# The decay of a state-space block computed as an absolute difference in PSUM, with the z gates moved and the preparation reordered

## What is computed

```python
def _ssd(xh, dt, A, Bm, Cm):
    cum = jnp.cumsum(dt * A, axis=1)
    diff = cum[:, :, None, :] - cum[:, None, :, :]
    decay = jnp.where(mask[None, :, :, None], jnp.exp(diff), 0.0)
    scores = jnp.einsum('bln,bsn->bls', Cm, Bm)[..., None] * decay * dt[:, None, :, :]
    return jnp.einsum('blsh,bshp->blhp', scores, xh)

def _mamba2(x, ...):
    z, xBC, dt = split(x @ Win)      # xBC: causal conv of 4 taps, silu; dt: softplus
    y = _ssd(xh, dt, A, Bm, Cm) + rev(_ssd(rev(xh), rev(dt), A, rev(Bm), rev(Cm)))
    y = y + D[None, None, :, None] * xh
    y = _rmsnorm(y * silu(z), gn_w)
    return x + y @ Wout
```

## Time and profile before

| what | value |
|---|---|
| median of three executions | 2949.18 us |
| profiled execution | 2953.49 us, its span 2951.5 us |
| blocks 0 to 7 | from about 904 us to 2929 us of the span |
| one block (the second) from its start to the start of the next | 248.4 us |
| busy in the span: TensorE, VectorE, ScalarE, GpSimd | 73%, 67%, 59%, 37% |
| mean granted clock of TensorE | 0.857 |

### The profile page before, as it was taken

How to read it: one execution, slowest core, us unless ns; L and a number is a source line. 1 busy time by engine, 2 the same in 40 slices (tenths; PEclk the granted TensorE clock), 3 DMA queues, 4 the chain that set the end, 5 groups by cost and what they waited for, 6 DMA issues and landing times. The chain is left out here.

```text
span 2951.5 us, 64266 instructions
## 1 busy us (share of the span) xinstructions
PE 2153.9 (73%) x26182; PEld 1100.1 (37%) x26182; DVE 1981.8 (67%) x2779; ACT 1744.2 (59%) x2811; POOL 1079.7 (37%) x827
## 2 busy tenths in 40 slices
PE   4277777776774887698688588658857886885886
PEld 3022222222221553354255245325524542552553
DVE  2587888888877566565666656565765666666564
ACT  1266766766653575477367457536754773674574
POOL 0044444444451343244045235304522531451342
PEclk6588888888896998799799799869978988997998
DMA  4000000000001111110111111011111101111111
GB/s 133 0 0 1 0 1 0 1 0 0 1 0 29 32 34 28 35 33 15 44 38 26 38 27 40 15 31 32 34 36 26 42 15 39 33 25 30 32 34 31
DMA packets 96695, 74.59 MB, mean 25 GB/s; under 512 B 69392, under 2 KB 77584, under 8 KB 95120
## 3 DMA queue, kind: packets, MB, share of 16 engines
q1 hardware_dynamic: 96400, 70.48, 10.0%
HBM read 20.62 MB, written 8.39 MB: 10 GB/s over the span
## 5 line engine op out<-in xcount | busy, mean ns | idle before, releaser
L892 POOL TENSOR_TENSOR SQ<-SQ 128x512 f32<-128x512 f32 x344 | 467.2, 1360 | 708.4 <-ACT SQ L811 425.1
L859 POOL TENSOR_TENSOR Y<-Z 128x512 f32<-128x512 f32 x256 | 330.8, 1292 | 531.6 <-DVE Z L1096 297.7
L807 ACT ACTIVATE O<-bank 128x512 f32<-128x512 f32 x512 | 304.3, 594 | 210.2 <-PE bank L571 207.5
L1293 DVE TENSOR_TENSOR SQ<-bank,O 128x512 f32<-128x512 f32 x344 | 236.2, 689 | 163.8 <-issue 118.8
L571 PE MATMUL bank<-SS,work 32*128 32x512 bf16 x512 | 203.7, 398 | 169.3 <-ACT O L807 168.2
L892 POOL TENSOR_TENSOR SQ<-O,SQ 128x512 f32<-128x512 f32 x168 | 226.9, 1350 | 254.8 <-PE bank L592 185.7
L1096 DVE TENSOR_TENSOR_SCAN Z<-bank,SS 128x512 f32<-128x512 f32 x256 | 311.0, 1215 | 0.5
L536 PE MATMUL bank<-folded_weights,work 128*64 128x128 f32 x4096 | 300.1, 292 | 0.0
L463 PE MATMUL bank<-Y,constants 128*128 128x512 f32 x512 | 295.5, 662 | 6.2 <-DVE bank L1104 4.6
L592 PE MATMUL bank<-folded_weights,work 128*32 128x64 f32 x8192 | 287.3, 230 | 11.3 <-POOL SQ L892 10.8
L512 PE MATMUL bank<-XP,block_weights 128*128 128x512 f32 x256 | 156.9, 725 | 174.3 <-DVE Z L1227 174.3
(11 more groups left out here) (271 smaller groups left out, 3990.2 us busy)
## 6 DMA issues: line engine op xcount, KB each, us to landing
work<-XP SPq DMA_DIRECT2D x256, 134.0 KB
work<-extra SPq DMA_DIRECT2D x768, 8.0 KB
decay_cols_kept<-extra SPq DMA_DIRECT2D x48, 128.0 KB, 1.8
SS<-decay_cols_kept SPq DMA_DIRECT2D x384, 16.0 KB
block_weights<-callw SPq DMA_DIRECT2D x8, 735.0 KB, 4.4
Z<-state_sel SPq DMA_DIRECT2D x1, 2048.0 KB, 13.2
out<-O SPq DMA_DIRECT2D x2, 1024.0 KB, 8.5
constants<-consts SPq DMA_DIRECT2D x1, 1347.5 KB, 6.1
```

The costliest lines, as they stand in the source:

```text
L807: A(D2C[u % 2], bank[2], ACT.Copy).then_inc(sg("d2_copied"), 1)
L859: g.tensor_tensor(hc[t_ % 4], hs[t_ % 4], c_copy[t_ % 4], ALU.mult).then_inc(sg("s1_hc"), 1)
L892: g.tensor_tensor(MM[u % 2].rearrange("p (h l) -> p h l", l=L), DK[u % 3].rearrange("p (h l) -> p h l", l=L), GM[(u // 8) % 2][:, 64 * (u ...
L1293: v.tensor_tensor(DK[u % 3], bank[u % 2], D2C[u % 2], ALU.min).then_inc(sg("decay_least"), 1)
```

## The change

With G = dt*A/2, H its running sum, M = 2H - G and C = log(dt) - G (with the constant that dL carries), the smaller of the two logarithms is G_l + C_s - |M_l - M_s|. Per step TensorE writes the difference to bank u%3 (`distance`), ScalarE takes Abs in place in PSUM, TensorE accumulates the offset on top (`decay_logs`), ScalarE takes Exp with scale -1 into DK in SBUF, and GpSimd multiplies with the scores as before, into three MM buffers instead of two. The copy to D2C, and VectorE's minimum in every step, are gone.

Three tiles M, G and C are split instead of four: ScalarE rounds, VectorE subtracts, GpSimd takes no part. Two sets of folded weights exist, and VectorE folds those of block c+1 inside block c (`fold`, pieces 0, 1, 2, 6 before the softplus, 3, 4, 5, 7 in slots -5 to -2); for block 0 it does all eight pieces ahead of the rounds. TensorE projects B, C and x of group 0 and all sixteen z ahead of the loop, ScalarE copies each z to SBUF (`copy_z`), and takes its tanh later, two in each eight slots (slots 0 and 1, `z_due`), from SBUF into bank 7. VectorE gates z in the same slots. One of the two squares also goes to bank 7, and Square waits for the gates of z. Six of the row DMAs of group 0 are issued by ScalarE. The scores are computed as sixteen matmuls of 32 by 64 in place of eight of 64 by 128; BB halves and gate_b is one instruction instead of two.

```diff
-        MM = [SQ[:, 2048 + 512 * i:2560 + 512 * i] for i in range(2)]
-        DK = [SQ[:, 3072:3584], SQ[:, 3584:4096], O[:, 3072:3584]]
+        MM = [SQ[:, 2048 + 512 * i:2560 + 512 * i] for i in range(3)]
+        DK = [SQ[:, 3584:4096], O[:, 2048:2560], O[:, 2560:3072]]
...
+        def z_due(tau):
+
+            i, r = divmod(tau, 8)
+            return 2 * i + r if r < 2 and 0 <= i < 8 else None
...
-                for k, (name, ready) in enumerate((("F", "split_F"), ("E", "split_E"))):
-                    sp.wait_ge(sg(ready), c + 1)
-                    for j in range(3):
-                        sp.dma_start(cols_dram[k, j], SPLIT[name][j]).then_inc(sg("decay_stored"), 16)
-                rows_of_decay(0)
+                keep(0, "M")
+                decay_rows(sp, 0, 0, "M")
+                keep(1, "G")
+                sp.wait_ge(sg("decay_stored_M"), (c + 1) * 48)
+                cols_of_decay(0, 0, "M")
+                sp.wait_ge(sg("decay_stored_G"), (c + 1) * 48)
+                cols_of_decay(0, 1, "G")
+                sp.wait_ge(sg("split_C"), c + 1)
                 rows_of_decay(1)
                 for g in range(2, NGROUP):
...
-                    t, to = z_place(i)
-                    if i >= 8:
-                        pe.wait_ge(sg("z_ready"), c * 16 + i)
-                    elif i >= 3:
-                        pe.wait_ge(sg("z_ready"), c * 16 + (i - 2))
-                    mm(bank[to], W(f"wz{i % 2}"), xn_group(i // 2), start=True, stop=True).then_inc(sg("z_psum"), 1)
+                    if i >= 5:
+                        pe.wait_ge(sg("z_copied"), c * 16 + (i - 4))
+                    mm(bank[z_banks[i % 5]], W(f"wz{i % 2}"), xn_group(i // 2), start=True, stop=True).then_inc(
...
                 def scores(g):
                     pe.wait_ge(sg("bc_ready"), c * 8 + g + 1)
                     for u in range(8):
-                        last = mm(bank[6][:, 64 * u:64 * u + 64], BB[0:64, 128 * u:128 * u + 128],
-                                  C2[0:64, 64 * u:64 * u + 64], start=True, stop=True, skip_group_check=True)
+                        for b in range(NB):
+                            h, a = slice(32 * b, 32 * b + 32), slice(64 * u, 64 * u + 64)
+                            last = mm(bank[6][64 * b:64 * b + 64, a], BB[h, a], C2[h, a], start=True, stop=True,
+                                      tile_position=(32 * b, 64 * b), skip_group_check=True)
...
-                def decay_logs(u):
+                def decay_matmul(u, k):
                     r = (u // 8) % 2
                     a = L * (u % 8)
+                    h = slice(32 * k, 32 * k + 32)
                     cols = RHS[r].rearrange("p (h n) -> p h n", h=8)[:, :, a:a + L]
-                    rows = LHS[r][:, 2 * a:2 * a + 128]
+                    return mm(bank[u % 3], LHS[r][h, 2 * a:2 * a + 128], cols[h, :, :], start=(k == 0), stop=(k == 1),
+                              tile_position=(32 * k, 0), skip_group_check=True)
+
+                def distance(u):
+                    r = (u // 8) % 2
                     if u % 8 == 0:
                         pe.wait_ge(sg(f"decay_cols{r}"), (c * 4 + u // 16 + 1) * 96)
                         pe.wait_ge(sg(f"decay_rows{r}"), (c * 4 + u // 16 + 1) * 192)
-                    if u >= 1:
-                        pe.wait_ge(sg("d2_copied"), c * L + u)
-                    mm(bank[2], rows[32:64, :], cols[32:64, :, :], start=True, stop=True,
-                       tile_position=(32, 0)).then_inc(sg("decay_logs2"), 1)
-                    if u >= 2:
-                        pe.wait_ge(sg("decay_least"), c * L + u - 1)
-                    mm(bank[u % 2], rows[0:32, :], cols[0:32, :, :], start=True, stop=True,
-                       tile_position=(0, 0)).then_inc(sg("decay_logs1"), 1)
+                    if u >= 3:
+                        pe.wait_ge(sg("decay_ready"), c * L + u - 2)
+                    decay_matmul(u, 0).then_inc(sg("distances"), 1)
+
+                def decay_logs(u):
+                    pe.wait_ge(sg("distance_abs"), c * L + u + 1)
+                    decay_matmul(u, 1).then_inc(sg("decay_logs"), 1)
...
+                    if 0 <= tau + 2 < L:
+                        decay_logs(tau + 2)
                     if 0 <= tau + 3 < L:
-                        decay_logs(tau + 3)
-                    for i in Z_SLOTS.get(tau, ()):
-                        z(i)
+                        distance(tau + 3)
                     for half in range(2):
...
+                def copy_z(i):
+                    act.wait_ge(sg("z_psum"), c * 16 + i + 1)
+                    A(Z2[:, z_at(i)], bank[z_banks[i % 5]], ACT.Copy).then_inc(sg("z_copied"), 1)
+
+                def round_high(name):
+                    act.wait_ge(sg(f"source_{name}"), c + 1)
+                    A(SPLIT[name][0], source[name], ACT.Copy).then_inc(sg(f"high_{name}"), 1)
+
+                def round_mid(name):
+                    act.wait_ge(sg(f"rest_{name}"), c + 1)
+                    A(SPLIT[name][1], left_over[name], ACT.Copy).then_inc(sg(f"mid_{name}"), 1)
+
+                for i in range(5):
+                    copy_z(i)
                 act.wait_ge(sg("dt_bounded"), c + 1)
                 A(dL, dL, ACT.Ln).then_inc(sg("dL_ready"), 1)
-                for j, (src, ready) in enumerate(((dE, "dE_ready"), (rest_e, "rest_E"))):
...
+                hbbc = folded(c)[7]
+                tanh_bc(0)
+                tanh_x(0)
+                act.wait_ge(sg("split_C"), c + 1)
+                decay_rows(act, 0, 1, "C")
+                for i in range(5, 16):
+                    copy_z(i)
 
                 for tau in range(FIRST, LAST):
...
                     u = tau + 2
                     if 0 <= u < L:
-                        act.wait_ge(sg("decay_logs2"), c * L + u + 1)
-                        if u >= 2:
-                            act.wait_ge(sg("decay_least"), c * L + u - 1)
-                        A(D2C[u % 2], bank[2], ACT.Copy).then_inc(sg("d2_copied"), 1)
-                    u = tau + 1
+                        act.wait_ge(sg("decay_logs"), c * L + u + 1)
+                        if u >= 3:
+                            act.wait_ge(sg("mixed"), c * L + u - 2)
+                        A(DK[u % 3], bank[u % 3], ACT.Exp, scale=-1.0).then_inc(sg("decay_ready"), 1)
+                    u = tau + 3
                     if 0 <= u < L:
-                        act.wait_ge(sg("decay_least"), c * L + u + 1)
-                        A(DK[u % 3], DK[u % 3], ACT.Exp).then_inc(sg("decay_ready"), 1)
-                    for i in Z_SLOTS.get(tau, ()):
-                        z(i)
+                        act.wait_ge(sg("distances"), c * L + u + 1)
+                        A(bank[u % 3], bank[u % 3], ACT.Abs).then_inc(sg("distance_abs"), 1)
                     k = every(tau, 4, -4, 16)
-                    if k is not None:
-                        act.wait_ge(sg("x_projected"), c * 16 + k + 1)
-                        if k >= 1:
-                            act.wait_ge(sg("x_ready"), c * 16 + k)
-                        A(TX, bank[3], ACT.Tanh, scale=0.5).then_inc(sg("x_tanh"), 1)
+                    if k is not None and k > 0:
+                        tanh_x(k)
                     g = every(tau, 8, -7, NGROUP)
-                    if g is not None:
-                        act.wait_ge(sg("bc_projected"), c * 8 + g + 1)
-                        if g >= 1:
-                            act.wait_ge(sg("bc_ready"), c * 8 + g)
-                        A(TBC, bank[6], ACT.Tanh, bias=hbbc, scale=0.5).then_inc(sg("bc_tanh"), 1)
-                        act.wait_ge(sg("bc_tanh"), c * 8 + g + 1)
-                        A(bank[6], bank[6], ACT.Identity, bias=W("bbc")).then_inc(sg("bc_biased"), 1)
+                    if g is not None and g > 0:
+                        tanh_bc(g)
+                    i = z_due(tau)
+                    if i is not None:
+                        act.wait_ge(sg("z_copied"), c * 16 + 16)
+                        if i >= 1:
+                            act.wait_ge(sg("z_ready"), c * 16 + i)
+                        if i >= 4:
+                            act.wait_ge(sg("scaled"), c * 8 + i // 2 - 1)
+                        A(bank[7], Z2[:, z_at(i)], ACT.Tanh, scale=0.5).then_inc(sg("z_tanh"), 1)
                     g = every(tau, 8, 10, NGROUP)
                     if g is not None:
                         act.wait_ge(sg("gated"), c * 16 + 2 * g + 2)
+                        act.wait_ge(sg("z_ready"), c * 16 + min(2 * g + 4, 16))
                         if g >= 1:
...
-                order = Order(pool, "split_order_p", c * 3)
-                hi, mid, lo = SPLIT["F"]
-                pool.wait_ge(sg("dF_ready"), c + 1)
-                order(g.tensor_copy(hi, dF))
-                order(g.tensor_tensor(rest_p, dF, hi, ALU.subtract))
-                order(g.tensor_copy(mid, rest_p))
```

(78 more changed lines are left out.)

241 lines of the change are left out of this document (110 added, 131 removed).

## The result

| | before | after |
|---|---|---|
| median | 2950.59 us (4 runs, 2942.47 to 2953.03) | 3040.21 us (4 runs, 3040.09 to 3040.28) |
| ratio | 1 | 1.031, 95% interval 1.0297 to 1.0323 |
| one block: dt to y(0) | 52.4 us | 40.4 us |
| one block: y(0) to y(63) | 171.2 us | 192.8 us |
| mean granted clock of TensorE | 0.857 | 0.836 |

Slower by 3.1%, 90 us, where 0.4% (2960 us) was forecast; the time lies 0.2 us outside the range. The preparation gave what was expected of it (12.0 us per block, 10.9 expected), the loop took more (21.6, 11.4 expected).

A forecast was written before the change was run, and what follows sets the result against it. The loop was taken as bound by TensorE with a little lock step. Per block, loop +11.4 and preparation -10.9 gave +0.5; eight blocks +4, block 0's folds +5, about +9 on the 2949.2 median: 2960 us, range 2870 to 3040.

The forecast's parts named there:

- The preparation: From the dt tile to the first y matmul: 41.5 us where it was 52.4, 10.9 us less per block.
- The lock step: Steady eight slots: TensorE waits 3.5 us for gate_x, behind gate_z waiting for its tanh; period 23.4 against 20.9 us.
- the scores: Score matmuls in the loop: 32 instructions on two tiles take 1.2 us, between 0.85 and 1.92, against 1.92 before.
- clock term: Main loop: each group's gap brings a TensorE stretch at 1.2 GHz; 1.6 us per group, bounds 0 and 3.3, 11.2 per block.
- The folds of block 0: Ahead of all rounds: folding the first block's weights stands there once, +5 us.
- Rival (e): ScalarE in the loop: Abs needs a table load beside Exp, some +900 us in all, 3850 us; chance 0.04.
- rival (d): Main loop: TensorE falls to 1.2 GHz twice per group, around the wait for gate_y's Square; 3020 to 3090 us, chance 0.22.
- the last seven steps 13.9: End of each block's loop: the last seven steps before y(63) take 13.9 us, clock left out.
- my recurrence: Steady eight slots: step times of TensorE, ScalarE and VectorE worked out from the decay pair; period 22.18 us plus scores.
- the cover of the logarithm and exponential: Output gate in the loop: Ln and Exp no longer start during the scores, standing behind Exp and Abs of slot 5.
- A gain in the preparation and a loss in the loop of equal size cancel: Whole block: preparation -10.9 us against y(0) to y(63) +11.4 us, +0.5 per block.
- own range: Main forecast's range, 2925 to 3000 us, chance 0.50: scores +-20, preparation +-16, clock +-28 us.

The follow-up runs named there:

- e3: Changed kernel plus three float32 matmuls, results unused, filling TensorE's gap in slot 2 of each of the first seven groups; 2910.28 us, ratio 0.9872.
- e7: Changed kernel plus ten short matmuls, results unused, in TensorE's waits of a block's last slots; 3012.19 us, ratio 1.021.
- e8: Changed kernel with the output gate's logarithm and exponential moved ahead of the decay's Exp on ScalarE, in slot 61 alone; 3012.03 us, ratio 1.0213.
- e2: Changed kernel with ScalarE's tanh of z moved ahead of tanh and bias of B and C; 2927.24 us, ratio 0.9932.
- e1: Changed kernel with VectorE gating x and y before z in a slot; 2748.49 us, ratio 0.932.
- e4: Changed kernel with the old scores, eight matmuls of 64 by 128, and the gate of B in two instructions; 3117.16 us, ratio 1.0579.
- e5: On top of e1, ScalarE copies z 5 to 9 ahead of its six row DMAs; 2723.16 us, ratio 0.9237.
- e6: On top of e1, Abs on one column of 512 and Exp scaled by -0.001, result not the reference's; 2634.37 us, ratio 0.8932.

## Why the prediction was wrong

**Right: the mechanism.** The lock step was worked out ahead and came as written: no minimum on VectorE, a wait of 3.52 us (3.5 predicted) of TensorE for the gate of x in each group but the last, behind a gate of z that waits for its tanh; the scores in 1.08 us (1.2 predicted, 1.92 in the earlier trace rows); Abs in PSUM 0.59 (0.55, from the earlier trace rows). Without its clock term the period was right too: 23.4 predicted, 23.4 in e3 (with the measured scores it would have been 23.3). By the rule of the Trainium skill that a change of the tiling mode drains TensorE (TensorEngine Tiling (Array Packing), Key Properties) the scores would have stayed near 1.9. They did not; a drain can have no more of the 1.08 than what exceeds the estimate of 0.85 for streaming alone, and no run shows it by itself. One sum is off by little: the prices listed for TensorE in eight slots add up to 18.6, not 18.4, against 18.52 busy.

**Right in size, in part by luck: the preparation.** dt to y(0) was 40.4 where 41.5 was predicted; an issue from ScalarE takes 0.72 us, close to SP's 0.74 that I had taken. Two misses inside it cancel. In TensorE's timeline:

```profile
1211.23 7.41 PE L524 MATMUL bank<-XP,block_weights 128*128 128x512 f32 x12 [10.65 <-ACT Z L807]
...
1222.00 1.91 PE L548 MATMUL bank<-folded_weights,work 128*64 128x128 f32 x16
...
1224.39 1.63 PE L548 MATMUL bank<-folded_weights,work 128*64 128x128 f32 x16
```

TensorE resumed 23.6 us after dt, not 24.9, and its last six z took 7.4, not 8.6, so the scores were done at 32.8 and not at 35.4. From the first distance to y(0) it then took 7.6 us, not 6.1: the half projections of x took 1.91 and 1.63 where 1.3 and 1.0 were forecast.

The folds of block 0 came out at +5 by luck alone. Its dt stands at 926.9 instead of 922.25, but VectorE spent 9.05 us on the folds (887.36 to 896.41). Stage 1, in which no instruction was changed, had ended 4.8 us earlier in this trace (887.3 against 892.1), and in the traces of the experiments it ends between 883.9 and 889.2. Why is open.

Rival (e) is dead: both kernels load tables as often, 64 times at each of the two lines of the output gate. The Trainium skill (ScalarE: Activation LUTs, Table sets) says abs is in every set; the trace agrees.

**The step that failed first: the size of the clock term.** "1.6 per group, bounds 0 and 3.3" was taken from a gap of 1.9 us, after which one stretch at 1.2 GHz of 3.4 us followed. After gaps of 3.52 the stretch covers one half projection of x or both, in turns from group to group, and groups of 24.9 and 26.1 to 26.2 stand beside the 23.4 of e3: 1.5 and 2.7 to 2.8 us. Why they alternate, no run shows. In the first seven groups of the second block the clock took 21.9 - 19.6 = 2.3, then 127.1 - 117.0 = 10.1, then 24.5 - 21.7 = 2.8, 15.2 in all where I had 11.2. The measured time lies in the range of rival (d), 3020 to 3090, chance 0.22, but not by its mechanism: TensorE did not fall twice in a group, its one stretch was longer in every other group.

**The step that failed most: "the last seven steps 13.9".** They took 19.4. The recorded forecast gives the 13.9 without its working. First, my recurrence had no gate of x in slot 57, but the sixteenth stands there, two instructions ahead of the gate of y, 1.4 us by the earlier trace rows; the squares wait for it, then Exp and Abs behind them: TensorE waits 2.39 us. Second, I gave these steps no clock term, though before the change they already ran at 0.88: from 1406.2 to 1420.4 the granted clock is 0.52; the sum of squares takes 2.08 us and the output projection 3.54. e7 gives 3.3 of the 5.5 us to this. Third, I had written that the cover of the logarithm and exponential was gone, and priced it for the steady group alone, where TensorE waits 0.37 us for it; in the last steps it makes the gap of 1.68 us, and e8, which closes it, gives back 3.2 us, in part the same ones. The gate of x in slot 57 has no run of its own: its 1.4 us are read from the timeline.

**The sum with the measured terms.** Per block +4.0 (clock in seven groups), +0.8 (the seventh group 21.7 for 20.9), +5.5 (last steps), -1.1 (preparation): +9.2, times eight 74 us. On the profiled execution's forecast of 2962.5 (2953.5 + 9) that is 3036; the profiled execution after took 3040.3. The remaining 4 us are about what the time from y(63) to the dt of the next block grew by, 0.9 to 1.0 us behind three of the blocks and 2.1 behind a fourth.

**The balance.** "A gain in the preparation and a loss in the loop of equal size cancel" was the bold sentence. Their sizes were not equal: -12.0 and +21.6. The doubt between 1.6 and 2.8 us per gap alone is worth 8 x 7 x 1.2 = 67 us, more than the +-28 that the own range of the forecast gave it.

## What to carry to other kernels

An in-order engine that is busy half of its time can still set the period: look at what stands first in its slot and what that waits for, and put the gate whose input is early ahead of the one whose input is late (here 292 us of 3040 for one move). Where a wait of some microseconds is forecast for TensorE, count both the wait and the work behind it at 1.2 GHz (15.2 us a block here), and take the last group, where no other work fills the waits, as a case of its own.

## What the runs showed of the hardware that was not expected

- After one and the same gap of 3.5 us the time at 1.2 GHz covered one half projection of x in one group and two in the next, there over 6.10 us (0.50), in all eight blocks. Gaps of 2.23 us (e2) brought groups of 22.1, 23.6 and 24.7 us in one block; waits of 0.59 us (e1) left 1.00.
- Scores as 32 instructions on two row tiles of 32 take 1.08 us, 16 on one tile of 64 by 128 take 1.93 (e4).
- A DMA issue from ScalarE costs 0.72 us of its sequencer, and its arithmetic goes on beside that only where it was queued ahead (3.24 us of ScalarE idle in the changed kernel; e5: three copies from 1165.82 to 1167.40, with an issue from 1166.27 to 1166.97 beside them).
- Abs from PSUM to PSUM takes 0.59 us for 128x512, 0.04 more than the Square of the earlier trace rows; on one column the wait behind it is 0.42 us shorter (e6).
